# Seven block products for each pair of output tiles, in a fused grouped convolution and gated low-rank layer

## The reference

```python
h = conv1d(x, weight, kernel 9, padding 4, 4 groups) + (c @ c_weight.T)[:, :, None] + bias   # (32, 64, 1024)
q = h @ Wq_w.T                       # 16 query values a row
scores = q @ keys.T                  # 64 experts
gate = softmax over the 16 largest scores, 0 for the others
z = (h @ A_w.T) * gate, each gate value for 8 columns     # 512 columns
out = x + 2.0 * (z @ B_w.T)          # 1024 columns
```

## Time and profile before

| what | value |
|---|---|
| median of 3 runs | 234.68 us (233.78 to 234.82) |
| profiled execution | 234.61 us, its span 232.8 us |
| TensorE busy | 228.6 us, 98% |
| VectorE busy | 172.9 us, 74% |
| ScalarE busy | 113.2 us, 49% |
| granted TensorE clock | 1.000 |

### The profile page before, as it was taken

How to read it: one execution, slowest core, us unless ns; L and a number is a source line. 1 busy time by engine, 2 the same in 40 slices (tenths; PEclk the granted TensorE clock), 3 DMA queues, 4 the chain that set the end, 5 groups by cost and what they waited for, 6 DMA issues and landing times.

```text
span 232.8 us, 4002 instructions
## 1 busy us (share of the span) xinstructions
PE 228.6 (98%) x1381; PEld 204.4 (88%) x1381; DVE 172.9 (74%) x411; ACT 113.2 (49%) x293; POOL 7.7 (3%) x16
## 2 busy tenths in 40 slices
PE   8999999999999999999999999999999999999995
PEld 8999998888989989898898989889898989898884
DVE  2699889999878696977969587786958748827232
ACT  4996768265282562728356272735627262221000
POOL 2010071000000000000000000000000000000000
DMA  6999055742825538164553815545381433552632
GB/s 186 373 400 398 34 136 184 290 115 102 235 117 145 175 98 260 58 177 181 137 182 91 270 50 167 192 134 187 89 271 52 117 109 90 184 175 98 182 134 92
DMA packets 23780, 38.79 MB, mean 167 GB/s; under 512 B 2768, under 2 KB 11856, under 8 KB 23760
## 3 DMA queue, kind: packets, MB, share of 16 engines
q1 hardware_dynamic: 23616, 38.45, 50.8%
q10 hardware_dynamic: 144, 0.08, 0.2%
HBM read 25.94 MB, written 12.58 MB: 165 GB/s over the span
## 4 chain that ended last, share of the span: by engine, by line
PE 77%; DVE 15%; issue 3%; DMA 2%; ACT 2%; SPq 1%; DVEq 0%; ACTq 0%
PE p_z L686 30%; PE p_out L724 12%; PE p_out L725 12%; PE p_out L732 12%; PE p_conv L637 10%; DVE h_lo L801 3%; DVE h_t L841 2%; DMA x_blk<-in_x_blocks 2%; DVE a_lo L801 2%; DVE x_lo L801 2%; DVE z_g L926 1%; DVE a_raw L936 1%; ACT h_c L426 1%; ACT x_hi L390 1%; DVE b_lo L801 1%
## 5 line engine op out<-in xcount | busy, mean ns | idle before, releaser
L724 PE MATMUL p_out<-b_hi,zt_hi 128*128 128x512 f32 (+1 forms) x128 | 50.8, 398 | 0.3 <-DVE x_nat L944 0.3
L725 PE MATMUL p_out<-b_hi,zt_lo 128*128 128x512 f32 (+1 forms) x128 | 50.0, 392 | 0.0
L732 PE MATMUL p_out<-b_lo,zt_hi 128*128 128x512 f32 (+1 forms) x128 | 34.3, 391 | 0.0
L686 PE MATMUL p_z<-a_hi,h_hi 128*128 128x264 f32 x240 | 34.1, 285 | 0.1
L686 PE MATMUL p_z<-a_hi,h_lo 128*128 128x264 f32 x240 | 34.2, 285 | 0.0
L686 PE MATMUL p_z<-a_lo,h_hi 128*128 128x264 f32 x240 | 34.0, 284 | 0.0
L686 PEld LDWEIGHTS p_z<-a_hi,h_hi 128*128 128x128 f32 x240 | 31.9, 188 | 1.9 <-issue 0.8
L686 PEld LDWEIGHTS p_z<-a_hi,h_lo 128*128 128x128 f32 x240 | 31.2, 188 | 0.0
L686 PEld LDWEIGHTS p_z<-a_lo,h_hi 128*128 128x128 f32 x240 | 31.1, 188 | 0.0
L724 PEld LDWEIGHTS p_out<-b_hi,zt_hi 128*128 128x128 f32 x128 | 24.1, 188 | 6.0 <-issue 0.4
L732 PEld LDWEIGHTS p_out<-b_lo,zt_hi 128*128 128x128 f32 x128 | 23.8, 188 | 5.7
(11 more groups left out here) (109 smaller groups left out, 280.1 us busy)
## 6 DMA issues: line engine op xcount, KB each, us to landing
x_nat<-in_x_rows SPq DMA_DIRECT2D x16, 512.0 KB, 5.2
out_dram<-x_nat SPq DMA_DIRECT2D x31, 256.0 KB, 3.0
x_blk<-in_x_blocks SPq DMA_DIRECT2D x14, 516.0 KB, 3.6
z_dram<-a_raw SPq DMA_DIRECT2D x64, 64.0 KB, 1.8
a_raw<-z_dram SPq DMA_DIRECT2D x16, 256.0 KB, 3.6
a_raw<-in_a_wq SPq DMA_DIRECT2D x8, 264.0 KB, 6.4
x_nat<-in_b_w SPq DMA_DIRECT2D x4, 512.0 KB, 9.1
x_blk<-in_x_blocks SPq DMA_DIRECT2D x2, 258.0 KB, 3.8
```

The costliest lines, as they stand in the source:

```text
L686: mm = nc.tensor.matmul(z_bank(t, b)[:, 0:HB], h[:, t % 2, r, :], a[:, r, b * HB:(b + 1) * HB], start=k == 0 and r == 0, stop=k == 2 and r ...
L724: nc.tensor.matmul(dst, zt_hi[:, t % 2, c, :], b_hi[:, c, cols], start=c == 0, stop=False)
L725: nc.tensor.matmul(dst, zt_lo[:, t % 2, c, :], b_hi[:, c, cols], start=False, stop=False)
L732: mm = nc.tensor.matmul(dst, zt_hi[:, t % 2, c, :], b_lo[:, c, start:stop], start=False, stop=c == JC - 1)
```

## The change

Tiles 4 to 13 are taken in five pairs m = 0 to 4, tiles 4+2m and 5+2m. The two tiles' z, each in two blocks of 256 columns, and B in 2 x 2 blocks make a 2 x 2 by 2 x 2 product of blocks, computed with seven block products (Winograd's form of Strassen's scheme) instead of eight. A block product is six matmuls (`product`). It needs four sums of z blocks for each pair (`sum_z31`, `sum_z2`, `sum_z4`, VectorE) with their splits (z1, z12, z34, z22), four sums of B blocks formed once, in the iterations 3 to 6 (`sum_b`, `split_bt`, 1024 elements each) from blocks of B that are loaded again, and running sums in PSUM: ScalarE copies a bank into the next one (`copy_xy`, `copy_yz`, `copy_zx`), and PE accumulates on it. The seven products end in x_nat through five adds: `add_5` (one bank into both tiles, 1024 elements), `add_11`, `add_12`, `add_22`, `add_21`. The pair's work is spread over an odd and an even iteration (m = (i-7)//2); the tiles 0 to 3, 14 and 15 go as before. In the iterations 5 and 6 only one half of tile 3 stands between the scores and the next z.

With it, `conv_sum(i + 2)` goes between the two banks of z from iteration 4 on; x blocks from tile 5 on are in two slots for three; the weights of groups 2 and 3 are loaded later; z's bank 0 and bank 1 wait for their own gate; the seven warm-up matmuls become one of 512 and three of 128 columns; `add(0, 0)` goes ahead of `split_h(4)`.

```diff
+FP = 4
+NP = (NT - 2 - FP) // 2
+TB = 3
+LD = FP + 2 * NP
...
+        XW = XS + XO
-        x_blk = sb("x_blk", [P, XB, XS + 2 * XO])
+        x_blk = sb("x_blk", [P, XB * XS])
...
-        zt_hi = sb("zt_hi", [P, 2, JC, P], F32R)
-        zt_lo = sb("zt_lo", [P, 2, JC, P], F32R)
+        zt_hi = sb("zt_hi", [P, 7, 2, P], F32R)
+        zt_lo = sb("zt_lo", [P, 7, 2, P], F32R)
+        bt_hi = sb("bt_hi", [P, 4, 2, J], F32R)
+        bt_lo = sb("bt_lo", [P, 4, 2, J], F32R)
...
+        def pair_banks(m):
+            if m == NP - 1:
+                return p_conv[:, 0, :], p_conv[:, 1, :], p_conv[:, 2, :], p_t[:]
+            return p_out[:, 0, :], p_out[:, 1, :], p_conv[:, 2, :], p_t[:]
...
+            sp.wait_ge(s_alo, R)
+            load_b(0, 0, 0)
+            load_b(1, 0, 1)
+            sp.wait_ge(s_tr, 2 * TW)
+            load_b(2, 1, 1)
+            for g in range(2, NG):
+                sp.dma_start(w_src(g), conv_w[:, g]).then_inc(s_w[g], 16)
             store(0, 0)
             for i in range(3, NT):
-                if i < NT - 2:
+                m = (i - FP - 3) // 2
+                if i == TB + 3:
+                    sp.wait_ge(s_btlo, 3)
+                    load_b(3, 1, 0)
...
+            def split_z12(m):
+                if m:
+                    act.wait_ge(s_p6, m)
+                act.wait_ge(s_zsum, 3 * m + 2)
+                high(zt_at(zt_hi, 2, 2), sums_at(1), s_z12hi)
...
+                if i >= FP + 4 and i % 2 == 0:
+                    copy_zx(m)
+                if FP + 3 <= i < NT - 1 and i % 2:
+                    copy_xy(m)
+                if i == NT - 2:
+                    copy_xy(NP - 1)
+                if i <= FP:
+                    split_z(i - 1)
+                if i == FP + 1:
+                    split_z1(0)
+                if i >= FP + 2 and i % 2 == 0:
+                    split_z12((i - FP - 2) // 2)
+                if FP + 3 <= i < NT - 1 and i % 2:
+                    split_z34(m)
+                    split_z22(m)
                 if i + 3 < NT:
                     split_x(i + 3)
...
                 if i + 2 < NT:
                     split_h(i + 2)
+                if TB <= i < TB + 4:
+                    split_bt(i - TB)
+                if FP + 3 <= i < NT - 1 and i % 2:
+                    split_z1(m + 1)
+                    copy_yz(m)
...
+            def product(dst, block, part, onto):
+                high, low = part
+                for c in range(2):
+                    nc.tensor.matmul(dst, zt_hi[:, block, c, :], high[:, c, :], start=c == 0 and not onto, stop=False,
+                                     skip_group_check=onto)
+                    nc.tensor.matmul(dst, zt_lo[:, block, c, :], high[:, c, :], start=False, stop=False, skip_group_check=onto)
+                for c in range(2):
+                    mm = nc.tensor.matmul(dst, zt_hi[:, block, c, :], low[:, c, :], start=False, stop=c == 1, skip_group_check=onto)
+                return mm
...
             for i in range(3, NT):
+                m = (i - FP - 3) // 2
                 for k in range(3):
                     z_product(i, k, (1,), range(R))
+                if TS <= i < NT - 2:
+                    conv_sum(i + 2)
                 z_product(i, 0, (0,), range(R))
                 z_product(i, 1, (0,), range(R))
                 if i < TS:
                     turn_q(i)
                 z_product(i, 2, (0,), range(R))
-                if i + 2 < NT:
+                if i < TS:
                     conv_sum(i + 2)
                 scores(i)
...
-                if i < NT - 1:
+                if i <= FP:
                     out_part(i - 2, 0)
-                if i + 2 < NT:
                     conv_pair(i + 2)
-                if i < NT - 3:
                     out_part(i - 2, 1)
...
+                elif i <= FP + 2:
+                    out_part(FP - 1, i - FP - 1)
+                    conv_pair(i + 2)
...
+                elif i % 2:
+                    product_1(m)
+                    product_5(m)
+                    conv_pair(i + 2)
+                    product_2(m)
+                    product_6(m)
+                else:
+                    product_7(m)
+                    product_3(m)
+                    conv_pair(i + 2)
+                    product_4(m)
...
+            add(0, 0)
             split_h(4)
-            add(0, 0)
...
+                if i == FP + 1:
+                    split_z1(0)
+                if TB <= i < TB + 4:
+                    sum_b(i - TB)
+                if i == FP + 2:
+                    sum_z31(0)
+                    add(FP - 1, 1)
+                    sum_z2(0)
+                    sum_z4(0)
+                elif i >= FP + 4 and i % 2 == 0:
+                    sum_z31(m + 1)
+                    add_12(m)
+                    sum_z2(m + 1)
+                    add_22(m)
+                    sum_z4(m + 1)
+                elif FP + 3 <= i < NT - 1:
+                    add_5(m)
+                    split_z34(m)
+                    split_z22(m)
+                    add_11(m)
+                if i >= FP + 2 and i % 2 == 0:
+                    split_z12((i - FP - 2) // 2)
                 if i + 3 < NT:
                     split_x(i + 3)
```

More of the change, by code:

```diff
@@ L259, in u_bank @@
         def u_bank(pair):
-            return p_z[:, 0, :] if pair else p_t[:]
+            return p_z[:, 1 - pair, :]
         def scores_at(t):
@@ L342, in _ @@
                 z_in(i)
[L343 to L351 removed]
+                if i <= FP + 1:
+                    store(i - 2, 0)
+                elif i == FP + 2:
+                    store(FP - 1, 1)
+                elif i % 2 == 0:
+                    store_half(m, 0, 1, s_c12)
+                    store_half(m, 1, 1, s_c22)
+                if i <= FP:
+                    load_rows(i + 1)
+                elif FP + 3 <= i < NT - 1 and i % 2:
+                    load_rows(i - 1)
+                    load_rows(i)
+            store_half(NP - 1, 0, 0, s_c11)
+            store_half(NP - 1, 0, 1, s_c12)
+            store_half(NP - 1, 1, 1, s_c22)
+            store(NT - 2, 0)
+            store_half(NP - 1, 1, 0, s_c21)
+            store(NT - 2, 1)
+            for k in range(len(parts(NT - 1))):
+                store(NT - 1, k)
             for k in range(XN):
@@ L675, in z_product @@
                         if t >= 3:
-                            pe.wait_ge(s_zg, 2 * t)
+                            pe.wait_ge(s_zg, 2 * t - 1)
+                    if k == 0 and 1 not in banks and t >= 3:
+                        pe.wait_ge(s_zg, 2 * t)
                     if k == 1 and 1 in banks:
@@ L739, in _, with product_3, product_4 @@
+            def product_3(m):
+                product(pair_banks(m)[1], 5, b_part(1, 1), True).then_inc(s_p3, 1)
+            def product_4(m):
+                pe.wait_ge(s_z22hi, m + 1)
+                pe.wait_ge(s_z22lo, m + 1)
+                pe.wait_ge(s_zx, m + 1)
+                product(pair_banks(m)[3], 6, b_sum(3, m), True).then_inc(s_p4, 1)
             pe.wait_ge(s_ones, 1)
-            for _ in range(7):
-                nc.tensor.matmul(p_t[:, 0:P], ones[:], ones[:], start=True, stop=True)
+            nc.tensor.matmul(p_t[:].rearrange("p (r n) -> p r n", n=P), ones, ones.unsqueeze(1).to_broadcast([P, 4, P]),
+                             start=True, stop=True)
@@ L742, in _ @@
+            for _ in range(3):
+                nc.tensor.matmul(p_conv[:, 2, 0:P], ones, ones, start=True, stop=True)
             products_u(0)
@@ L864, in split_keys, with sum_b, split_bt @@
+            def sum_b(k):
+                dst, other = ((0, 1), (0, 2), (1, 2), (0, 1))[k]
+                for load in ((0, 1), (2,), (), (3,))[k]:
+                    dve.wait_ge(s_bt[load], 16)
+                nc.vector.tensor_tensor(b_sums[dst], b_sums[dst], b_sums[other], ALU.add).then_inc(s_btsum, 1)
+            def split_bt(k):
+                dve.wait_ge(s_bthi, k + 1)
+                low(bt_lo[:, k], b_sums[(0, 0, 1, 0)[k]], bt_hi[:, k], s_btlo)
             def split_keys():
@@ L1065, in _ @@
                     split_h(i + 2)
-            add(NT - 3, 1)
+                if TB <= i < TB + 4:
+                    split_bt(i - TB)
+                if FP + 3 <= i < NT - 1 and i % 2:
+                    split_z1(m + 1)
+                if i == NT - 2:
+                    split_z22(NP - 1)
+                    add_21(NP - 2)
+            add_5(NP - 1)
+            add_11(NP - 1)
+            split_z(NT - 2)
+            add_12(NP - 1)
+            add_22(NP - 1)
             split_z(NT - 1)
             add(NT - 2, 0)
+            add_21(NP - 1)
             add(NT - 2, 1)
```

354 lines of the change are left out of this document (288 added, 66 removed).

## The result

The median went from 234.59 us (233.78 to 234.82) to **251.77 us** (250.78 to 253.88): the ratio of the times is 1.0751, with a 95% interval from 1.0678 to 1.0824. Forecast were 241.2 us and a range up to 246.0. So the direction was right, and the loss is over twice the size forecast. The profiled execution is the shortest of the four, 250.78 us with a span of 249.0 and a mean granted clock of 0.966; the other three had 0.959.

A forecast was written before the change was run, and what follows sets the result against it. TensorE was taken to bound the kernel, busy 98% of the span. 234.6 - 7.0 (products saved) + 6.0 (x_lo waits in iterations 8, 10, 12) + 3.1 (iteration 5) + 4.5 (iteration 6) = 241.2 us; range 235.0 to 246.0, chance 0.80.

The forecast's parts named there:

- What the products save: PE's output products: seven products of six matmuls for eight, 1.40 us a pair, five pairs, -7.0 us.
- the tail: Behind the last scores: both kernels have 19.8 us of PE work, so the 22.7 us there stay.
- The waits in front of x_lo: PE at the conv sum: 3.1 us in iteration 5, 4.5 in 6, 2.0 each in 8, 10, 12, nothing in odd ones.
- The first rival: PE waits only where VectorE's whole work exceeds PE's iteration; order inside an iteration is harmless; 233.5 us, chance 0.12.
- The query chain as next in line: `turn_q` to scores: covered by the x_lo wait; if that went away, a wait near 1.2 us in even iterations.
- PE's own way to the third product in the iterations 5 and 6: Conv sum between z's banks: PE reaches its third product, and wants x_lo, at T+7.65 (T: the iteration's scores matmul).
- half of the waits: Rival: prices of the added VectorE work near the lower bound, 234.6 - 7.0 + 7.5 = 235.1 us, no change; chance 0.06.
- The spacing of VectorE's instructions: Consecutive VectorE instructions start 0.60 us apart at 512 elements, 1.10 at 1024, taken from the profile's rows.
- The rule's 242.7 us: The skill's 691 ns for 512 elements as spacing: each added VectorE op some 0.09 us more, total near 242.7 us.
- The loads and copies set to nothing: B's reloads taken as 0 (bounds 0 and +3 us); ScalarE's bank copies cost nothing; `add_5` at 1.10 us.
- the clock follows the waits: Rival: PE at 1.2 GHz for the 24 matmuls behind each of two waits, 5.8 us more, 247.0 us; chance 0.05.
- A later x_lo and a slow restart: At the conv sum: x_lo at T+10.75 in iteration 5, T+11.04 in 8, 10, 12; PE takes it a hand-over (0.06) later.

The follow-up runs named there:

- e9: e7 with each GpSimd sum of B held until the iteration's second `differ` is done, and B's first two loads issued earlier; 232.67 us, ratio 0.9922 to the kernel before.
- e3: Changed kernel with the split of x put ahead of the sums on VectorE and ScalarE, in iteration 5 and even ones from 6; 237.64 us, ratio 1.0131.
- e2: Changed kernel with the conv sum moved back behind both banks of z in all iterations; 241.87 us, ratio 1.0298 to the kernel before.
- e1: Changed kernel with idle, never read matmuls put where PE waits for x_hi and x_lo (also called the filled kernel); 243.99 us, ratio 1.0399.
- e8: Changed kernel with x_hi ahead of the z12 split on ScalarE alone, in even iterations 6 to 12; 245.09 us, ratio 1.044 to the kernel before.
- e7: e6 with the split of x first behind the transposes in odd iterations too; 233.55 us, ratio 0.9935 to the kernel before.
- e5: e3 with the four sums of B and their four lo splits moved to GpSimd; 243.0 us, ratio 1.0355 to the kernel before.
- e6: e3 with only the four sums of B on GpSimd, their lo splits on VectorE; 233.32 us, ratio 0.9949 to the kernel before.

## Why the prediction was right or wrong

- **What the products save: right.** e9's stretches 10 and 12 last 12.43 us against 13.65, 1.22 us less where 1.40 were computed; the tail kept 22.7 us, and taking e9's three long stretches down to PE's work gives 227.9 against 227.6 computed.
- **The waits in front of x_lo: right in place and near in size, but for iteration 3.** Iteration 5: 3.10 us (3.1 forecast). Iteration 6: 3.24 + 0.57 us (4.5). Even iterations: 0.80 + 1.06 (2.0). Odd ones: 0.17 in iteration 7 (0). Iteration 3: 0.81 us, taken as nothing beyond the 0.3 us saved at the start. ScalarE's 5.05 us for `sum_z2` is the mechanism named, and e3 shows it from the other side: with x ahead of the sums, the even waits vanish. The first rival, in which the order inside an iteration is harmless, falls with that.
- **The query chain as next in line: right.** e2 uncovers it, with 1.65 us in stretch 8 where near 1.2 was given.
- **Two slips in the sums, neither of weight.** PE's own way to the third product in the iterations 5 and 6 is 10.51 - 2.80 = 7.71, not 7.65, and half of the forecast waits is 6.8, not 7.5, which puts the rival "half of the waits" at 234.4 us, below the range.
- **The spacing of VectorE's instructions: the row held.** They start 0.60 us apart again (133.64 to 134.24). The rule's 242.7 us was nearer to the result, but not for its reason.
- **The loads and copies set to nothing: right.** No wait of PE, VectorE or ScalarE on the reloaded B limits an iteration (its loads into a_raw land in 3.7 us at the median), a copy from bank to bank takes 0.58 us and lies where ScalarE waits anyway, and `add_5` is followed after 1.13 us (1.10 taken).
- **The clock: this is the step that failed.** The sum took every matmul behind a wait at the full clock. The rival "the clock follows the waits" had a chance of 0.05, on the argument that conv products lie between the parts of a wait. In iteration 5 only the last conv product was late, so PE stood for the 3.10 us in one piece, and in iteration 6 the clock was at 0.50 when the first product behind the 3.24 us ran. The rival was also priced for two places alone. It struck at four: behind 0.80 + 1.06 us too, in the iterations 10 and 12. That its 5.8 us came near the 6.8 measured is luck: at the two places priced the clock cost 1.50 + 2.13 = 3.6 us, and 3.1 at the two others. With the clock kept up (e1), the same waits give 243.99 us, inside the range that ends at 246.0.
- **A later x_lo and a slow restart: terms taken too small, 2.6 us.** In the filled kernel, with the clock at 1.000, the stretches still come to 153.8 against 151.2 forecast. Each stretch with a wait is 0.35 to 0.5 us longer than forecast and the odd ones behind about 0.2 (0.4 in iteration 7). The forecast resumed PE at full pace; in the rows the first matmul behind a wait is followed after 0.34 us (90.62 to 90.96; in e1 91.03 to 91.37) where 0.233 is the spacing, 0.1 us a wait. The rest is that x_lo came later than forecast. PE starts on it at T+11.20 in iteration 5 and at T+11.36 in iteration 8, where the forecast has 10.81 and 11.10. In iteration 8 VectorE is through with the transposes at T+5.83, not at T+5.59: the add that is gone saved 0.38 us and not 0.60, as the rows of MATCH_REPLACE8 and MAX8 show. In iteration 5 it is through with them at T+6.56, not at T+6.19. These parts are read from the rows; no run took them apart.

The sum as it should have been: 241.2 + 2.6 (the later x_lo and the restarts) + 6.8 (clock) = 250.6 us, against 250.8 in the profiled execution.

The Trainium skill (TensorE: Matmul & The Clock Gate, "Part 1: The HAM clock gate") says that PE without work falls back to 1.2 GHz, and its section "HAM oscillation — how this bites in real kernels" tells of a kernel whose waits for data throttle it again and again. The trace agrees, down to the level: a granted clock of 0.50 between 106.0 and 108.4 us, and 1.76 us for eight matmuls of 264 columns that took 0.97 at the full clock. The prediction cited the first of these sections and gave it little weight; its only trace held no wait over 1.0 us that could have spoken for or against it.

## What to carry to other kernels

When a change makes TensorE stand in an iteration for as long as here (1.86 to 3.8 us), price the wait and, beside it, the matmuls behind it at half the clock, as a case with a real chance; idle matmuls in the wait show in one run which of the two it is. In in-order queues the place of new work can count more than its amount, as it did here: the same instructions made this kernel 17 us slower than before in one order, and 3 us slower with the split that TensorE waits for put ahead of them (e3). Work handed to GpSimd should start where VectorE's next instructions have one input or read PSUM: those kept their length beside it, though no run here shows how much of the total the choice of place is worth.

## What the runs showed of the hardware

- **The clock after short waits.** It fell behind 3.10 us, behind 3.24 + 0.57, and behind 0.80 + 1.06 with two conv products between them in the iterations 10 and 12, but not behind the same waits in iteration 8, nor behind a single wait of 1.45 us in e8. The other runs are as mixed: it fell behind waits of 1.87 (e2), 1.91 (e7), 2.58 (e3) and 3.17 us (e5), and not behind 1.85 (e3) nor behind 1.01 and, one conv product later, 2.17 us (e2). So the length of a wait alone does not decide it here; what does, and what tells iteration 8 from 10, stays open.
- **Filling a wait paid.** 47 more matmuls in e1 (1392 for 1345), never read, took 7.8 us off the median.
- **GpSimd holds VectorE.** An instruction of 64 elements took 2.44 us beside a GpSimd add of 1024. Seen lengthened were instructions with both operands in SBUF (x_blk differences, h_lo, `split_q`, `e_top`, k_r); a one-input transpose beside it kept 0.21 us, and an add with one operand in PSUM its 0.68. GpSimd's own instructions of 1024 elements took 2.4 us where they held VectorE or met none of these, and up to 3.22 in e5. The Trainium skill (SBUF — State Buffer, "SBUF: two separate sides") says that a VectorE instruction with two SBUF inputs and a GpSimd one take the shared port pair by turns, each for its whole length. The traces of e5, e6 and e9 agree: e5's h_lo ends at 64.68, behind GpSimd's 63.60 by one length of its own.
